# Attention: the spread of the state factors moved from between scores and the projection of C to behind the second tile's scan

## The reference

```
xn = layernorm(x)
proj = xn @ W_in.T                     # xp 512 | z 512 | B 256 | C 256 | dt_low 16
dt = softplus(dt_low @ dt_W.T + dt_b)  # 16 heads
dAcs = cumsum(dt * -exp(A_log)) within chunks of 64 tokens
y_intra = sum_j (C_i . B_j) * exp(dAcs_i - dAcs_j) * causal * dt_j * x_j
state   = exp(dAcs_last) * state + sum_k B_k * dt_k * exp(dAcs_last - dAcs_k) * x_k   # chunk to chunk
y_cross = C_t . state * exp(dAcs_t)
y = (y_intra + y_cross + xp * D) / rms * norm_w * silu(z);   attn = y @ W_out.T
ffn: in groups of 32 tokens, for each of 128 (expert, set) the token with the largest logit is picked,
     run through a small two-layer network and scattered back
out = x + attn + ffn
```

## Time and profile before

| | |
|---|---|
| median of 3 runs | 3028.83 us (3025.64 to 3034.0) |
| profiled execution | 3038.94 us, its span 3036.7 us |
| granted clock of TensorE, mean | 0.988 |
| PE busy | 2889.0 us, 95% |
| PE weight loads | 2466.2 us, 81% |
| DVE busy | 2056.6 us, 68% |
| ACT busy | 1697.8 us, 56% |
| POOL busy | 1426.6 us, 47% |

### The profile page before, as it was taken

How to read it: one execution, slowest core, us unless ns; L and a number is a source line. 1 busy time by engine, 2 the same in 40 slices (tenths; PEclk the granted TensorE clock), 3 DMA queues, 4 the chain that set the end, 5 groups by cost and what they waited for, 6 DMA issues and landing times.

```text
span 3036.7 us, 134102 instructions
## 1 busy us (share of the span) xinstructions
PE 2889.0 (95%) x59304; PEld 2466.2 (81%) x59304; DVE 2056.6 (68%) x2980; ACT 1697.8 (56%) x3678; POOL 1426.6 (47%) x2287
## 2 busy tenths in 40 slices
PE   7999999999999999999999999997777778999999
PEld 5888888888888888888888888885666667888887
DVE  5777777777777777777777777674444447777775
ACT  5566665666656666566665666653333323555555
POOL 3666666666666667676666766662000001000000
PEclk9999999999999999999999999998999999999999
DMA  4222222222222222222222222216344436877765
GB/s 144 69 80 70 80 74 72 81 70 80 74 78 76 70 80 74 78 75 70 79 74 77 76 74 76 74 40 248 111 127 109 113 100 199 232 217 229 225 203 156
DMA packets 365218, 328.93 MB, mean 108 GB/s; under 512 B 56400, under 2 KB 278096, under 8 KB 363744
## 3 DMA queue, kind: packets, MB, share of 16 engines
q1 hardware_dynamic: 363712, 320.15, 35.5%
q10 hardware_dynamic: 928, 0.20, 0.0%
HBM read 206.96 MB, written 113.31 MB: 105 GB/s over the span
## 4 chain that ended last, share of the span: by engine, by line
PE 90%; DVE 4%; issue 4%; POOL 1%; DMA 1%; ACT 0%; SPq 0%; POOLq 0%; DVEq 0%; ACTq 0%
PE a_proj L920 40%; PE a_mix L920 12%; PE s_rt L1589 8%; PE g_pick_ps L1335 5%; PE a_scan L1031 5%; PE s_w_ps L1559 4%; PE s_rt L1602 4%; DVE g_picked L1302 3%; PE a_scan L1008 3%; PE g_acc_ps L1356 2%; PE a_scan L995 2%; PE a_mix L983 2%; PE a_misc L976 1%; PE a_misc L1049 1%; PE a_misc L1039 0%
## 5 line engine op out<-in xcount | busy, mean ns | idle before, releaser
L920 PE MATMUL a_proj<-wdh,xTh 128*128 128x512 f32 x1024 | 420.9, 411 | 6.2 <-ACT raw L586 5.6
L1525 ACT COPY s_res<-s_rt 128x512 f32<-128x512 f32 x512 | 262.9, 600 | 278.6 <-PE s_rt L1589 278.6
L920 PE MATMUL a_proj<-wdh,xTl 128*128 128x512 f32 x1024 | 403.0, 394 | 2.5 <-issue 2.5
L920 PE MATMUL a_proj<-wdl,xTh 128*128 128x512 f32 x1024 | 402.0, 393 | 0.0
L1538 DVE TENSOR_TENSOR s_resT<-s_w_ps,s_b 128x1024 f32<-128x1024 f32 x252 | 296.7, 1218 | 140.7 <-PE s_w_ps L1559 140.7
L766 DVE COPY_PREDICATED scan_in<-mask,a_scan 64x512 f32<-64x512 uint32 x512 | 379.4, 741 | 16.0
L444 POOL TENSOR_TENSOR dx<-xs,d_row 64x512 f32<-64x512 f32 x256 | 330.8, 1292 | 15.1
L622 ACT ACTIVATE scan_in<-CT,hsel 64x128 f32<-64x128 f32 x1024 | 326.1, 388 | 4.8
L452 POOL TENSOR_TENSOR yv<-yt,dx 128x512 f32<-128x512 f32 x128 | 188.9, 1476 | 294.2 <-DVE yt L806 294.2
L1302 DVE COPY g_picked<-g_pick_ps 128x1024 f32<-128x1024 f32 x128 | 156.7, 1224 | 230.3 <-PE g_pick_ps L1335 230.3
L586 ACT ACTIVATE raw<-a_proj,rs 128x272 f32<-128x272 f32 x128 | 62.3, 488 | 428.2 <-PE a_proj L920 428.2
(11 more groups left out here) (138 smaller groups left out, 7294.2 us busy)
## 6 DMA issues: line engine op xcount, KB each, us to landing
x<-in_x_dram SPq DMA_DIRECT2D x128, 256.0 KB, 2.6
xn_dram<-xn SPq DMA_DIRECT2D x128, 256.0 KB, 2.4
part_dram<-res SPq DMA_DIRECT2D x128, 256.0 KB, 2.6
g_xn<-xn_dram SPq DMA_DIRECT2D x128, 256.0 KB, 2.9
s_w<-in_w_dram SPq DMA_DIRECT2D x128, 256.0 KB, 3.9
s_part<-part_dram SPq DMA_DIRECT2D x128, 256.0 KB, 3.6
out_dram<-s_out SPq DMA_DIRECT2D x128, 256.0 KB, 2.9
xr<-in_xT_dram SPq DMA_DIRECT2D x126, 256.0 KB, 2.8
```

Source lines behind the costliest of these rows:

```text
L920: last = nc.tensor.matmul(out, lhs[a], rhs[c], start=(k == 0 and n == 0), stop=(k == nk - 1 and n == 2))
L1525: nc.scalar.copy(res[:, n % 4, :, :], rt_bank[:, n % 3, :, :]).then_inc(res_cp, 1)
```

## The change

On PE, spread_gains(s) leaves its place between the scores of the second tile and the projection of C, and becomes the last call of the step, behind the scan of the second tile. On ACT, the copy of the factors to mg goes from before copy_c(s) to the end of the step, behind square(n1, 0). On DVE, picks(s) (and, in step 0, the low part of the last weight stage) go ahead of last_decay(s) and the last states operation. No instruction is added or taken away on any engine.

```
@@ scalar_program
             if valid(s + 1):
                 normalize(2 * (s + 1) + 1)
             if valid(s):
+                copy_c(s)
+                silu_z(n0 + 1)
+            if valid(s - 1):
+                square(n1, 0)
+            if valid(s):
                 act.wait_ge(mg_ps, s + 1)
                 wait(act, decayed, 2 * (s - 1))
                 nc.scalar.copy(mg[:, par, :, :], misc[:, GAINS:GAINS + 8 * NG].rearrange("p (g c) -> p g c", g=NG)).then_inc(mg_ready, 1)
-                copy_c(s)
-                silu_z(n0 + 1)
-            if valid(s - 1):
-                square(n1, 0)
@@ vector_program
             if valid(s - 2):
                 residual(n2 + 1, 1)
+            if s == 0:
+                stage_lo(LAST_STAGE)
+            if valid(s):
+                picks(s)
             if valid(s - 1):
                 if valid(s):
                     last_decay(s)
                     states(n1 + 1, 1, second, fresh=s % STB == 0)
-            if s == 0:
-                stage_lo(LAST_STAGE)
-            if valid(s):
-                picks(s)
@@ tensor_program
             if valid(s):
-                spread_gains(s)
                 project_c(s)
                 project_z(n0 + 1)
...
             if valid(s - 1):
                 scan(n1 + 1)
+            if valid(s):
+                spread_gains(s)
```

More of the change, by code:

```diff
@@ L693, in scalar_program @@
             if valid(s):
-                act.wait_ge(mg_ps, s + 1)
-                wait(act, decayed, 2 * (s - 1))
-                nc.scalar.copy(mg[:, par, :, :], misc[:, GAINS:GAINS + 8 * NG].rearrange("p (g c) -> p g c", g=NG)).then_inc(mg_ready, 1)
                 copy_c(s)
@@ L700, in scalar_program @@
                 square(n1, 0)
+            if valid(s):
+                act.wait_ge(mg_ps, s + 1)
+                wait(act, decayed, 2 * (s - 1))
+                nc.scalar.copy(mg[:, par, :, :], misc[:, GAINS:GAINS + 8 * NG].rearrange("p (g c) -> p g c", g=NG)).then_inc(mg_ready, 1)
     def vector_program(dve):
@@ L910, in vector_program @@
                     states(n1 + 1, 1, second, fresh=s % STB == 0)
[L911 to L914, removed]
     def tensor_program(pe, gather):
```

## The result

The changed kernel took 3061.3 us (median of 4 runs, 3058.35 to 3065.11) against 3030.36 us for the kernel before (4 runs). The ratio is 1.0097, 95% interval 1.0082 to 1.0112: 31 us slower. I had forecast 3022.8 us, with 0.06 for a loss by instruction loading and 0.10 for any loss above 0.3%. The profiled executions are 3038.94 and 3060.2 us, with spans of 3036.7 and 3058.0: 21.3 us apart, as that of before was 8.6 us above its own median. What follows accounts for the 21.3 us, not for the whole 31.

A forecast was written before the change was run, and what follows sets the result against it. PE's own stream was taken to bound each step. Steps -8.2, step 0 +0.3, tail +0.7 and loading +1.2 made -6.0 us, from a median of 3028.83 to 3022.8 us, range 3014 to 3034.

The forecast's parts named there:

- the term for instruction loading: PE's instruction queue, scan and spread now adjacent: irregular stops estimated to cost +1.2 us in all, between -5 and +5.
- the -5 end: Favourable bound on instruction loading: the 4.9 us of stops at projections behind the scan vanish.
- the rival of a bigger gain: Saving per step as worked out, and stops just behind the scan vanish: -12 us, 3016.7 us; chance 0.26.
- the 4.9 us at projections behind the scan: Irregular "issue" stops of PE at projections, taken to stand exactly where the spread moves; 4.9 us in all.
- The old place gave back 0.40 us and the new one cost 0.27: PE, per step: 0.40 us saved between scores and projection, 0.27 added behind the second scan; -0.13 over 63 steps.
- No idle ahead of the spread: PE behind the second scan: the spread follows without idle, adding 0.27 us; with an idle of 0.17, 0.44.
- The cost on ACT and on DVE at nothing: Late factor copy on ACT and later scaling of y on DVE stay hidden, 0 us; 0.9 us in hand at dA.
- The tail: First step after the last projection: chunk states wait for y's scaling, which comes 0.75 us later; +0.7 us.
- Slower, by loading: A packet boundary within the burst comes too soon, stopping PE 0.8 us every second step: +18 us, 3047; chance 0.06.
- Slower, by DVE: Scaling of y comes later than worked out, dA late by 0.3 us each step: +13 us, 3042; chance 0.04.
- -10.7 us for 63 steps: PE saving by the skill's rule: one tiling mode change fewer per step at 0.17 us; not used in the sum.
- The rows made -8.2: PE saving by the profile's rows: 63 steps at -0.13 us each, the forecast's first term.

The follow-up runs named there:

- e9_waits_good: Changed kernel with PE's step cut to 1152 instructions by leaving out implied waits, and 12 small matmuls ahead of the first step: 3015.81 us, ratio 0.9924.
- e6_before_waits_good: Kernel before with PE's step cut to 1152 instructions by leaving out implied waits, and 13 small matmuls ahead of the first step: 3021.0 us, ratio 0.9946.
- e1_pe_back: Changed kernel with the spread back in its old place on PE, ACT and DVE in the new order: 3032.84 us, ratio 1.0013.
- e5_len_bad: Changed kernel with sums as 2 matmuls of 64 columns (1152 instructions a step) and 4 small matmuls ahead of the first step: 3148.84 us, ratio 1.0366.
- e4_len_good: Changed kernel with sums as 2 matmuls of 64 columns (1152 instructions a step) and 16 small matmuls ahead of the first step: 3022.53 us, ratio 0.9974.

## Why the prediction was wrong

*The step that failed* is the term for instruction loading in the sum: +1.2 us, with -5 and +5 as ends. The stops over 0.4 us went from 12.7 to 37.7 us, +25.0. Counted from the first undisturbed start of the sums to the last (61 steps), the changed kernel takes 1957.03 us, of which 61 x 31.33 are regular and 45.9 irregular; the kernel before 1931.62, with 16.2 irregular at 31.40. So loading costs 29.7 us: 25.0 of stops and, by the clock records, 13.7 us at half clock in place of 3.4, which is some 5.1 lost (together 30.1, 0.4 more than counted). The shorter regular step gives back 4.3, and the rest of the program is 4.1 us shorter in this profile: +21.3.

Where the reasoning went astray can be named. I had the mechanism (a packet is about 250 instructions, the densest stretch is behind the move, it was a rival with its price) and took "the nearest row stops rarely" for a property of the stretch. I didn't ask what the stops have in common from one to the next. The trace held it: 384.94 and 1934.17 in the earlier trace rows are two of 12 stops, and the one at 384.94 comes again at 1396.05, 32 steps and just 145 blocks of 256 later, at the same instruction of a step. With 1160 instructions a step, the mark visits every eighth place of a block of 256 in turn. A stretch of R dense instructions can hold a whole block in about (R - 256) / 8 of 32 steps. The traces have stops in 6 of 32 for the 281 of sums and first scan, in none for the 257 at the second scan of before, and in 9 for the 321 there after the change, 16 in 62 steps; so the formula gives what the change adds there (8), but not each count (3 for the 281). At 1.06 us each, the mean of the 12 stops of before, 16 make 17 us and a sum of +10, slower by 0.3%, all from the trace of before. Their true size, 1.6 us each, and the clock behind them could not be read there.

A reading went wrong too, and it carried the -5 end and the rival of a bigger gain: the 4.9 us at projections behind the scan. They do not stand at the place that the edit changes. All four are behind the first tile's scan, and they are all still there after the change.

*Other steps.* The old place gave back 0.40 us and the new one cost 0.27 (1.50 in place of 1.23 us from the scan's start to the projection): -0.13, measured on segments; the whole regular step is -0.11 us in e9_waits_good against e6_before_waits_good. In the changed kernel itself it is only -0.07; in its undisturbed steps the projection behind the first scan takes 2.67 us where it takes 2.63 in both fixed versions. I have not settled why. No idle ahead of the spread: right. The cost on ACT and on DVE at nothing: right (e1_pe_back within 0.13%, dA with 0.92 us in hand). The tail looks too small: from the last scan that has a projection ahead of it to the next chunk states it is 4.53 us in place of 3.25, +1.28 where I had +0.7. But 1.79 of it is a wait that ends at 2075.00, at a mark and 1.41 us behind the end of a q8 transfer: a packet stop again. In e9_waits_good, which has none there, the stretch is 4.03 us, +0.78. So this term was right, and the rest belongs to the loading.

*The rivals.* "Slower, by loading" happened, with a stop in every second step in the bad part of the drift and none in the good, not an even 0.8 us. I gave it 0.06. Its price, +18 us, is near the +21.3 of the profiled executions, but that is partly luck: it had 31 stops of 0.8 us where 16 of 1.6 came, and nothing for the clock. "Slower, by DVE" didn't, with the order that the change has; with DVE's old order it would have cost 66 us, so the reordering of DVE is what keeps the late spread cheap.

*The two pages.* The rule of the Trainium skill, TensorEngine Tiling (Array Packing), section Tiling Modes, that a change of mode drains the engine, at the 0.17 us of the rows, made -10.7 us for 63 steps in the prediction. The rows made -8.2, and -6.9 are measured (63 x 0.11). The Trainium skill, Runtime: NRT & Kernel Launch, section Instruction fetch mechanics, calls the crossing of a block "mostly hidden". The traces agree as far as the number goes, with 12 stops over 0.4 us at 277 marks before and 28 at 272 after, but the few that aren't hidden decide this case.

## What to carry to other kernels

Where an engine's stream is packed with tiny instructions, count them. Find the stops whose reason is "issue", see whether their place in the instruction count repeats modulo a packet, and look at the instruction queue's transfers: here each stop ended 1.2 to 1.7 us behind one. Price a move by how many more places of the packet fit wholly into the dense stretch, not by how often it stopped before. If the loop is written out with a fixed length, a few instructions more or less per step can make that length a multiple of half a packet, and a few ahead of the loop choose the places: here worth 0.5% on the old order, where the reordering itself is worth 0.2%. The good places are not those outside the dense stretch; a mark in the first few loads of it did no harm, with long matmuls in front, and one from the 12th load or so on cost up to 3.0 us. And when a producer is moved late, see that what doesn't need it goes ahead of it on the consumer's queue.

## What the runs showed of the hardware

- PE's irregular stops are waits for its next packet of 256 instructions. All 234 over 0.4 us at a mark, in nine kernels, ended 1.19 to 1.66 us behind the end of a q8 transfer; at 3308 other marks, in all thirteen, the load ran no sooner than 1.24 us behind it.
- In the stops at the spread of e5_len_bad, 3.3 to 4.2 us lay between the mark in the scan and the end of the stop. At 1012.54 it was 3.60: 1.23 to the start of the transfer, 0.93 for it, 1.44 behind it. PE needs 1.2 us of that for the 256 instructions; the stop is the rest.
- This is no least time for 256 instructions. In e4_len_good and e9_waits_good, some 30 times each, they were used in 1.08 to 1.20 us without a stop, as the transfer had begun 1.2 to 2.0 us ahead of the mark's load. So the request for a packet can run ahead of the engine's work while long matmuls are in front. How far it can, in instructions, no run here measured.
- Stops of 1.7 us and more were followed at times by a granted clock of half, 1.2 GHz, with PE busy: 51.2 us of it in the steps of e5_len_bad, behind 13 of 29 stops, none in those of e4_len_good. In the kernel before it came once, behind the longest stop of the earlier trace rows.
- 12 small matmuls more or less, run once before the loop, changed the time by some 4% (3148.84 and 3022.53 us).
- Loads of the spread and of the scan, both 128*32, were merged at the seam (1301.31 to 1301.32 above). With 64-column loads in the sums in place of 32-column ones, the sums took 0.17 us more to the scan (0.31 and 0.14 us).
